# Row sums of a causal attention: pairs of probability tiles added by GpSimd before their product with ones

## What is computed

```python
scores = jnp.einsum('bhqd,bkd->bhqk', q, k) * scale
causal = jnp.tril(jnp.ones((S, S), dtype=bool))
scores = jnp.where(causal, scores, jnp.finfo(scores.dtype).min)
attn = jax.nn.softmax(scores, axis=-1)
out = jnp.einsum('bhqk,bkd->bhqd', attn, v)
out = out.transpose(0, 2, 1, 3).reshape(B, S, D)
out = rmsnorm(out, w_pre)
return out @ Wo.T
```

## Time and profile before

| | |
|---|---|
| median of 3 runs | 1219.67 us (1219.08 to 1219.68) |
| the profiled execution's own time | 1219.15 us |
| its span, first to last instruction | 1217.4 us |
| TensorE busy (matmul) | 1161.7 us, 95% |
| VectorE busy | 975.9 us, 80% |
| ScalarE busy | 760.7 us, 62% |
| GpSimd busy | 493.7 us, 41% |
| attention with all that lies beside it | from about 60 us to 650 us |
| experts | from about 692 us to the end |

### The profile page before, as it was taken

One profiled execution on the slowest core, in us unless ns is written; L12 is line 12 of the kernel. 1 busy time (PEld: TensorE's weight loads), 2 busy tenths in 40 slices (PEclk: granted clock), 3 DMA queues, 4 the chain that ended last, 5 costly groups with the idle time before them and its releaser, 6 DMA issues.

```text
span 1217.4 us, 25541 instructions
## 1 busy us (share of the span) xinstructions
PE 1161.7 (95%) x8905; PEld 877.7 (72%) x8905; DVE 975.9 (80%) x1881; ACT 760.7 (62%) x1507; POOL 493.7 (41%) x375
## 2 busy tenths in 40 slices
PE   8988999999999989999998999999999999999996
PEld 4455666555565555565557899999999999999983
DVE  4677787766657889786677889999999999999977
ACT  3456555556665535546754477777777777777741
POOL 1122222111122111111010248888878788778741
PEclk9999999999999989999999999999999999999999
DMA  9480000000000000004003279999999999999988
GB/s 348 152 333 1 1 10 10 10 10 2 15 10 10 10 1 23 1 10 115 23 21 124 84 212 297 302 298 302 295 300 296 298 295 297 301 300 294 299 238 294
DMA packets 75167, 189.95 MB, mean 156 GB/s; under 512 B 11544, under 2 KB 12184, under 8 KB 74832
## 3 DMA queue, kind: packets, MB, share of 16 engines
q1 hardware_dynamic: 44704, 116.27, 28.2%
q0 software_dynamic: 28672, 71.32, 23.7%
q10 hardware_dynamic: 1712, 1.32, 0.3%
HBM read 136.36 MB, written 52.51 MB: 155 GB/s over the span
## 4 chain that ended last, share of the span: by engine, by line
PE 71%; DVE 13%; DVEq 4%; issue 4%; ACT 4%; DMA 2%; POOL 1%; POOLq 0%; SPq 0%; ACTq 0%
PE ps L1349 22%; PE ps L1388 12%; PE ps L1168 8%; PE ps L1335 5%; PE ps L1153 4%; PE ps L1198 4%; PE ps L1113 4%; PE ps L1081 3%; DVE nmax L1631 2%; PE ps L1138 2%; DMA acc_dram<-y,slots 1%; DVEq L1705 1%; PE ps L1216 1%; PE ps L1185 1%; PE ps L1053 1%
## 5 line engine op out<-in xcount | busy, mean ns | idle before, releaser
L751 POOL DMA_INDIRECT acc_dram<-y,slots x128 | 249.6, 1950 | 78.1 <-issue 50.7
L1631 DVE TENSOR_REDUCE nmax<-ps 128x1 f32<-128x512 f32 (+3 forms) x304 | 190.8, 656 | 80.3 <-PE ps L1117 43.0
L860 ACT ACTIVATE probs<-ps 128x512 f32<-128x512 f32 (+1 forms) x320 | 159.0, 555 | 85.5 <-PE ps L1153 82.4
L702 POOL TENSOR_SCALAR_AFFINE_SELECT probs<-probs 128x512 f32<-128x512 f32 x64 | 43.1, 675 | 351.6 <-ACT probs L860 351.6
L736 POOL DMA_INDIRECT xg<-h_dram,slots x128 | 130.4, 1019 | 84.5 <-DVE slots L1822 40.5
L1113 PE MATMUL ps<-kpad,qpT 128*128 128x512 f32 (+3 forms) x384 | 144.5, 444 | 9.9 <-DVE nmax L1631 7.9
L1349 PE MATMUL ps<-x_hi,e_gu_hi 128*112 128x256 f32 (+1 forms) x768 | 120.1, 278 | 0.0
L1349 PE MATMUL ps<-x_hi,e_gu_lo 128*112 128x256 f32 (+1 forms) x768 | 119.6, 278 | 0.0
L1153 PE MATMUL ps<-qT,kT 98*128 98x512 f32 (+1 forms) x320 | 111.8, 428 | 2.6 <-ACT probs L860 1.9
L1349 PEld LDWEIGHTS ps<-x_hi,e_gu_hi 128*112 128x112 f32 (+1 forms) x768 | 105.7, 179 | 5.9
L1349 PE MATMUL ps<-x_lo,e_gu_hi 128*112 128x256 f32 (+1 forms) x768 | 109.9, 279 | 0.0
(11 more groups left out here) (238 smaller groups left out, 2409.1 us busy)
## 6 DMA issues: line engine op xcount, KB each, us to landing
e_gu<-in_gate_up SPq DMA_DIRECT2D x64, 704.0 KB, 7.4
e_d<-in_w_down SPq DMA_DIRECT2D x64, 224.0 KB, 4.7
acc_dram<-h SPq DMA_DIRECT2D x2, 4608.0 KB, 25.8
e_d<-in_w_down SPq DMA_DIRECT2D x64, 128.0 KB, 5.4
wmod_b<-in_wmod SPq DMA_DIRECT2D x2, 2048.0 KB, 23.6
xg<-h_dram SPq DMA_DIRECT2D x16, 256.0 KB, 6.6
acc_a<-acc_dram SPq DMA_DIRECT2D x8, 512.0 KB, 10.9
acc_b<-acc_dram SPq DMA_DIRECT2D x8, 512.0 KB, 6.6
```

The source lines that it names most:

```text
L751: pool.indirect_dma_start(out=acc_dram[a], out_offset=bass.IndirectOffsetOnAxis(ap=slots[:, at:at + 1], axis=0), in_=y[e % 2][:, h, :], in ...
L860: act.activation(probs[:, n % PROBS, 2 * pr:2 * pr + 2, off:CW], unit_bank(2 * n + pr)[:, :, off:CW], ACT.Exp).then_inc(s_exp, 1)
L1631: dve.tensor_reduce(nmax[:, 1 if lo else 0, first:first + heads], max_view(n, heads, hi - lo), AX.X, ALU.max, negate=True).then_inc(s_max, 1)
```

## The change

For a pair of key tiles that is not the group's last (the last is the diagonal one), the product with ones is not made of the two tiles but of their sum. GpSimd makes the sum of both tiles of all 4 heads in one instruction, 128x1024 (`pair_sum`), into one of two slots of a new tile `p_sum`. TensorE multiplies it with ones behind the values of the following pair. All products with values and the products of the diagonal pair with ones stay. There are 4 x (0+1+2+3) x 2 = 48 such pairs: 4 in q1 and in q5, 8 in q2 and q6, 12 in q3 and q7. Each has 8 products fewer and 4 new ones.

New waits: GpSimd waits for the exponentials of the pair and, from the third sum on, for the reader of the slot (`s_pv`); TensorE waits for the sum (`s_psum`); ScalarE's exponential into a slot of `probs` waits also for the sum that read the slot. To make room for `p_sum` (8 KB in each partition) the buffer for GpSimd's DMA descriptors is created with 8192 bytes in each partition; without the argument it is 16384.

```diff
+        p_sum = sb(att, "p_sum", [P, 2, GH, CW])
...
+        SUM_LAG = 0
...
+        def sums_before(q, g, k):
+
+            return sum(NG * (keys(i) // 2 - 1) for i in range(q)) + g * (keys(q) // 2 - 1) + k
...
+            def pair_sum(q, g, k):
+                n, c = step_of(q, g, 2 * k), sums_before(q, g, k)
+                pool.wait_ge(s_exp, 2 * n + 4)
+                if c >= 2:
+                    pool.wait_ge(s_pv, sum_read(c - 2))
+                pool.tensor_tensor(p_sum[:, c % 2, :, :], probs[:, n % PROBS, :, :], probs[:, (n + 1) % PROBS, :, :],
+                                   ALU.add).then_inc(s_psum, 1)
+
...
                 for q, g, kt in steps_at(m):
                     if kt >= keys(q) - CT:
                         causal(q, g, kt)
+                for q, g, kt in steps_at(m, SUM_LAG):
+                    if kt % 2 and kt < keys(q) - CT:
+                        pair_sum(q, g, kt // 2)
                 for tile, _ in due(m, "head_rms"):
                     head_rms(tile)
...
                 if n >= PROBS:
                     act.wait_ge(s_pv, (n - PROBS) // 2 + 1)
+                    if kt % 2 == 0:
+                        before = sums_done(n - PROBS + 1)
+                        if before > sums_done(n - PROBS - 1):
+                            act.wait_ge(s_psum, before)
...
-                for at in (0, CW):
+                for kt in (2 * k, 2 * k + 1):
+                    off = first_query(q, kt)
+                    for j in range(GH):
+                        last = pe.matmul(ps[HD * j:HD * j + HD, PV_BANK, off:CW], v_sb[:, b, kt, :],
+                                         probs[:, (n + kt % 2) % PROBS, j, off:CW], start=(kt == 0), stop=False)
+                if k:
+                    c = sums_before(q, g, k - 1)
+                    pe.wait_ge(s_psum, c + 1)
+                    for j in range(GH):
+                        last = pe.matmul(ps[HD * j:HD * j + HD, PV_BANK, CW:2 * CW], ones[:, :], p_sum[:, c % 2, j, :],
+                                         start=False, stop=False)
+                if k == last_pair:
                     for kt in (2 * k, 2 * k + 1):
                         off = first_query(q, kt)
                         for j in range(GH):
-                            last = pe.matmul(ps[HD * j:HD * j + HD, PV_BANK, at + off:at + CW],
-                                             v_sb[:, b, kt, :] if at == 0 else ones[:, :],
-                                             probs[:, (n + kt % 2) % PROBS, j, off:CW], start=(kt == 0 and at == 0),
-                                             stop=(kt == keys(q) - 1 and at == CW))
+                            last = pe.matmul(ps[HD * j:HD * j + HD, PV_BANK, CW + off:2 * CW], ones[:, :],
+                                             probs[:, (n + kt % 2) % PROBS, j, off:CW], start=False,
+                                             stop=(kt == keys(q) - 1))
                 last.then_inc(s_pv, 1)
...
-    nc = bacc.Bacc("TRN2", target_bir_lowering=False, num_devices=1)
+    nc = bacc.Bacc("TRN2", target_bir_lowering=False, num_devices=1, dynamic_dma_scratch_size=8192)
```

More of the change, by code:

```diff
@@ L282, in build_program @@
         s_sc, s_exp, s_mask, s_pv, s_on, s_div = (sem("s_" + n) for n in ("sc", "exp", "mask", "pv", "on", "div"))
+        s_psum = sem("s_psum")
         s_rec, s_t2, s_hi2 = (sem("s_" + n) for n in ("rec", "t2", "hi2"))
@@ L404, in step_of, with sums_done, sum_read @@
             return steps_before(q) + g * keys(q) + kt
+        def sums_before(q, g, k):
+            return sum(NG * (keys(i) // 2 - 1) for i in range(q)) + g * (keys(q) // 2 - 1) + k
+        def sums_done(n):
+            found = 0
+            for q in range(NCHUNK):
+                for g in range(NG):
+                    found += sum(step_of(q, g, 2 * k + 1) <= n for k in range(keys(q) // 2 - 1))
+            return found
+        def sum_read(c):
+            for q in range(NCHUNK):
+                pairs = NG * (keys(q) // 2 - 1)
+                if c < pairs:
+                    g, k = divmod(c, keys(q) // 2 - 1)
+                    return step_of(q, g, 2 * k) // 2 + 2
+                c -= pairs
         def masks_before(q, g, kt):
```

## The result

The changed kernel takes 1269.33 us, the median of 4 runs (1259.45 to 1269.83), against 1219.38 us (1218.94 to 1219.68) for the kernel before, run beside it: 1.0399 times as long, interval 1.0375 to 1.0423. The forecast was 1227 us with a range of 1210 to 1240. The sign was right, the size was not.

What follows compares the result with a forecast made beforehand. TensorE was taken to bound q2, q3 and q6, VectorE q5, with both on q7's chain. 1219.15 us less 14.2 of products plus 21.8 of VectorE waits gave 1226.8, said as 1227 us; range 1210 to 1240.

Steps and rivals of the forecast that it cites:

- What is taken from TensorE: Off-diagonal pairs' products with ones: 0.44 us less for each of 48 pairs, 21.1 us, of which 14.2 us on the chain.
- What the sum costs GpSimd: Each pair sum on GpSimd takes 2.3 us, 48 sums 110 us; ready before TensorE's read in all 48.
- What the sum costs VectorE, the laying out: Two-input VectorE instructions starting inside a GpSimd sum wait for its end: 36 of 48 sums, 51 us together.
- What the sum costs VectorE, how much reaches the end: By VectorE's room in each stage, 21.8 us of the waits reach the end, bounds 0 and 51 us.
- Other edits, the clock: New TensorE stalls can bring more lower-clock stretches, 3.4 us of work each; none counted, one more in the range.
- The descriptor buffer: In the experts' part the smaller buffer could make GpSimd wait for descriptors; cost 0, or 26 us if not hidden.
- All is passed on: Rival: held VectorE delays row maxima for TensorE; 27 us loss plus 5 for delays and a clock stretch, 1237.5 us; chance 0.23.

Runs made afterwards that it cites:

- The zeros: The changed kernel with the products of before and no sum read, GpSimd filling both slots of p_sum with zeros where it added: 1226.35 us, ratio 1.0064.
- the row of sixteen: The changed kernel with each sum made by sixteen GpSimd instructions of 64 elements, in all chunks: 1254.87 us, ratio 1.0308.
- the products alone: The kernel before, with the product with ones of an off-diagonal pair taking only its first tile and nothing added by GpSimd: 1204.65 us, ratio 0.9885.
- four parts: The changed kernel with each sum made by four GpSimd instructions of 256 elements, one for each head: 1234.93 us, ratio 1.0153.
- the additions alone: The changed kernel with its GpSimd additions, but TensorE multiplying both tiles with ones as before and nobody reading the sums: 1269.83 us, ratio 1.0426.

## Why the prediction was wrong, step by step

- *What is taken from TensorE*: right, 14.2 us predicted, 14 measured (interval 10 to 18), and the split by stage too. The share of a line on the chain of waits times its share of the line's work was a good estimate, as long as nothing else moved. Beside the additions the same saving gave nothing (1269.83 us without it, 1269.33 with it), and the prediction had simply added the two terms.
- *What the sum costs GpSimd*: right, 2.37 us for 2.3. The sums are ready in time, also as said.
- *What the sum costs VectorE, the laying out*: 36 of 48 and 51 us were predicted; 42 of 48 and 65 us (616.9 - 552.3) came. The casts were missing from my list, since I had seen only two-input instructions held. The Trainium skill (SBUF — State Buffer, "SBUF: two separate sides") has both kinds: an instruction of VectorE in a two-port performance mode, or one with two SBUF inputs, the latter only against a GpSimd instruction that reads. The zeros show just this, cast 2.0 us, multiplication unchanged. Its "whole instruction" holds for the additions; in the row of sixteen a few holds went on over several instructions.
- *What the sum costs VectorE, how much reaches the end*: this failed. I passed on 21.8 us; TensorE stood 38 us more. By stage, against the run with the products alone (the holds against the kernel before):

| us | q1 | q2 | q3 | q5 | q6 | q7 |
|---|---|---|---|---|---|---|
| hold, predicted | 5.2 | 5.7 | 7.9 | 6.8 | 9.8 | 15.9 |
| hold, measured | 4.8 | 8.5 | 16.7 | 5.8 | 8.9 | 19.5 |
| passed on, predicted | 2 | 1 with q3 | | 6.8 | 3 | 9 |
| TensorE standing, added | 4.5 | 4.7 | 2.7 | 6.3 | 5.8 | 14.1 |
| the clock: half of the work added at 0.50 | 5.0 | 10.1 | 1.7 | 0.8 | 3.1 | 5.4 |

In q5, which VectorE bounds, the pass-on came out as said. The error was to set a hold against the idle time of a whole stage ("q2 and q3 have 23 and 33 us of idle VectorE: 1 left"). q3 did take up most of its hold, but q2 passed on half, q6 two thirds and q1 nearly all. The timeline at 248.70 shows how, for one of them: the hold falls in front of a row maximum, and TensorE has three banks between it and the wait, however much VectorE idles later. So what stands behind the held instruction has to be looked at, and the idle sum does not bound the loss. Over all chunks TensorE's added standing was about half of the total hold, whether one hold was up to 0.6 us (23 of 42) or up to 2.2 us (38 of 65); that a shorter hold by itself passes on a smaller share is not shown.
- *Other edits, the clock* ("I count none, and one more in the range"): this failed too, and is the larger surprise. Stretches at half clock went from 20.5 to 85.3 us, and cost 26 us. The trace of before had five such stretches up to the first gather, of which I showed one, and that was the warning. The two failed steps are the miss: 1227 + 16 (38 for 21.8) + 26 = 1269.
- *The descriptor buffer*: nothing, as said. The experts' part is 528.8 us for 528.6 and the scatters stand 79.0 us for 78.1.
- *Rivals*: "All is passed on" had the mechanism (queue in order, three banks, first wait not made good) and named a clock stretch, but took 27 and 5 us for what was 38 and 26. With those it gives 1219.7 - 14.2 + 64 = 1269.5.

What stays open: which of the stretches at half clock follows from which wait, since the same program gave 10 us more or less of time between executions; why the same standing (67.6 and 70.3 us) came with half as much work at half clock in the run with sixteen parts; whether the 38 us would be smaller at full clock; and what let VectorE in after ten additions in a few places and after one in most.

## What to carry to other kernels

Moving elementwise work to GpSimd beside a busy VectorE is not free because GpSimd is idle: count every VectorE instruction that reads SBUF twice, and every SBUF-to-SBUF cast, as blocked for the rest of a GpSimd addition or copy, and look at what waits behind it in the queue. Cut such an instruction into pieces, but not too small, since VectorE is then held for the rest of a piece only and the total hold shrinks (65 us with whole additions, 42 with four parts). Here, in q2, q3 and q6, pieces of 0.7 us left 7 of the 10 us that the shorter products alone gave there, and pieces of 1.35 us none; whole additions in all stages cost 65 us. Do it only in stages where VectorE does not bound. Where a trace already has stretches at the lower clock, put a term for the clock beside new waits of TensorE: 38 us of them brought another 26 here, 34 us brought 15 with the additions alone, and 23 us brought 4 to 5 with four parts (half of 24.7 - 15.8), so the runs give no fixed rate.

## What the runs showed of the hardware that I had not expected

- A GpSimd instruction that only writes SBUF (1.81 us) holds VectorE's fp32 cast from SBUF to SBUF, longest 2.006 us for 0.43, and not a two-input multiplication (0.798 us, as before).
- GpSimd's addition costs 2.37, 1.35, 0.73 and 0.32 us (medians or means) for 1024, 512, 256 and 64 elements of a partition: some 0.18 us and 2.1 ns an element. VectorE does the 1024 in 1.22 us, GpSimd's copy in 1.04.
- Short GpSimd instructions back to back do not always give VectorE its turn between them: with 0.3 us ones most holds ended within 0.2 us, but one 0.42 us instruction took 3.56 us. With 0.73 us ones the longest hold was 0.58.
- One program, two executions: 1259.45 us at a mean granted clock of 0.973 and 1269.83 at 0.963.
